# Loading the stacks of images 0 and 1 behind the last scores in a fused attention and convolution kernel

## The chip, the cores and the metric

The kernel runs on one core of one Trainium2 chip, as a single launch. The metric is the device time of a launch in microseconds (us), the median of several runs. All data are 32-bit floats.

## The reference

Two blocks follow each other on four images of 24 channels and 64 x 64 pixels. The first is a shifted-window transformer block with a gated convolution, the second a graph convolution with a small MLP.

```python
# x: (4, 24, 64, 64)
# block 1
xn  = layernorm over channels of x, gain norm1_g, shift norm1_b
q, k, v = windows of 8x8 of xn rolled by (-4, -4), 3 heads of 8 channels
att = softmax(q k^T / sqrt(8) + bias[rpb_table] + shift mask)
x   = x + unroll(att v @ proj_w.T + proj_b)
y   = layernorm over channels of x, gain norm2_g, shift norm2_b; its
      (positions, channels) are read on as (channels, rows, columns)
y   = conv1x1(y, pin_w)                  # 24 -> 126
y   = depthwise conv3x3(y, dw_w)         # padded by zeros
y   = gelu(y[:63]) * y[63:]
x   = x + conv1x1(y, pout_w)             # 63 -> 24
# block 2
h   = bn(conv1x1(x, w1))
xj  = max(0, h - rolls of h by even steps along rows, along columns)
h   = gelu(bn(conv1x1(concat(h, xj), wg)))
h   = bn(conv1x1(h, w2)) + x
out = conv1x1(gelu(conv1x1(h, wf1)), wf2)
```

## The kernel before

The kernel is written engine by engine: each engine has its own stream of instructions in a fixed order, and semaphores tie them. Its time has three stages, attention, convolution and the second block.

**Attention** runs over eight chunks m = 0 to 7 of 512 positions of all four images. Each chunk has four tiles t = 4m to 4m + 3. For a tile TensorE makes the scores (L595), VectorE adds the bias and takes the row maxima (L1065, L1069), GpSimd subtracts them (`subtract_max`, L496), TensorE transposes (`turn`, L606), ScalarE takes the exponential (L893) and TensorE multiplies by the values (`mix`, L624). Per chunk there follow the transposed output (L634), its projection (`project`, L641) and the residual. The second layer norm of chunk m runs some two chunks later: `turn_x1(m)` on TensorE (L578), `centre(1, m)` and `variance(1, m)` on VectorE, the square and the root on ScalarE (L930, L933), `gain(m)` (L453) and `second_norm(m)` (L466, L471) on GpSimd. For chunks 6 and 7 GpSimd takes the root itself with a power (L462), and VectorE's `variance(1, 7)` waits for the power of chunk 6.

The normalised chunk goes from SBUF to `scratch` in DRAM (`store_y(m)`, L273 or L275 to L277); the residual goes into the tile `x1` (`store_x1(m)`). Chunks 2b and 2b + 1 hold image b.

**Convolution.** `pin_w` and the 3 x 3 taps are folded into one product over a stack of shifted copies of an image: 12 channels times nine shifts are 108 partitions, and two stacks, sta and stb, hold the 24 channels. `load_stack(b, h)` loads half h of image b from scratch, with three DMAs into sta and three into stb (L292). A copy shifted in this way has wrong values at the image's borders, and GpSimd sets those to zero (`edges(b, h)`, L484): it waits for sta, multiplies three strips by 0 or 1, then the same for stb. `convolve(u)` on TensorE takes u = 8b + c, chunk c of image b (L650 on sta, L651 on stb); before u = 0, 4, 8, 12 and so on it waits for the edges of that half. It also waits for `gate(u - 4)`, so that its PSUM bank is free: ScalarE's gelu (L968) and VectorE's product (L1192) read it. convolve(0) to convolve(3) lie between the last steps of attention. From u = 25 on `pout_w` and the first product of block 2 are mixed in.

Images 0 and 3 share the buffers of the stacks, so `load_stack(3, 0)` waits until four chunks are convolved. Image 2's stacks lie over tiles of attention, so its load waits for the last scores. SP issues all loads and stores of these stages in one queue, in the order in which its program is written; GpSimd's order is written by hand too. TensorE's own instructions are fetched through a DMA queue of their own, which the trace lists as q8.

**Second block.** It is a pipeline over eight chunks at the end and is not touched.

Of the kernel before, what the change touches and what calls it, by code (L numbers as in the profile page):

```python
# [22 lines left out]
NCH = NT // CH  # L23
# [42 lines left out]
def build(nc, xw, xt, feat, pack, out):  # L66
    scratch = nc.dram_tensor("scratch", [B, PAD + C * NT + PAD], F32, kind="Internal").ap()

    with ExitStack() as ctx:
# [156 lines left out]
        def chunk(buf, n):  # L226
            return buf[:, bass.ts(n, CH)]
# [31 lines left out]
        def store_y(queue, m):  # L259
            b, i = divmod(m, 2)  # L260
            queue.wait_ge(y_ready, m + 1)
            tokens = scratch[b, PAD:PAD + C * NT].rearrange("(t c) -> t c", c=C)

            def rows_of(row, groups):
                part = tokens[W * row:W * (row + 8 * groups)]
                return part.rearrange("(g p k) c -> p g (k c)", g=groups, k=TOK)

            def half_of(row):
                return tokens[W * row:W * (row + 4)].rearrange("(p k) c -> p (k c)", k=TOK)

            done = y_stored[i]
            if i:
                queue.dma_start(rows_of(32 - SHIFT, 4), ytok[:, 1]).then_inc(done, 16)  # L273
            else:
                queue.dma_start(rows_of(8 - SHIFT, 3), ytok[:, 0, 1:4]).then_inc(done, 16)  # L275
                queue.dma_start(half_of(H - SHIFT), ytok[0:64, 0, 0]).then_inc(done, 16)
                queue.dma_start(half_of(0), ytok[64:128, 0, 0]).then_inc(done, 16)  # L277

        def load_stack(queue, b, h, paced=False):

            half = NT // 2
            for n in range(2):
                c0, c1 = STACKS[n]
                for y in range(3):
                    if paced and (n or y):
                        at, before = divmod(3 * n + y - 1, 3)
                        queue.wait_ge(stack_in[at][b][h], 16 * (before + 1))
                    src = scratch[b]
                    off = PAD + (y - 1) * W - 1 + c0 * NT + half * h
                    src = bass.AP(src.tensor, src.offset + off, [[NT, c1 - c0], [1, 3], [half // 2, 2], [1, half // 2]])  # L290
                    dst = stack(n, b)[y:RS:3, half * h:half * h + half].rearrange("p (q n) -> p q n", q=2)
                    queue.dma_start(dst, src).then_inc(stack_in[n][b][h], 16)  # L292
# [35 lines left out]
        @block.sync  # L328
        def _(sp):
            p0, p1, p2, p3 = PACK_LOADS  # L330

            def load_tokens(m):
                if m >= RING:
                    sp.wait_ge(cen_ready, m - RING + 1)
                sp.dma_start(xtok[:, m % RING], xt[:, GR * C * m:GR * C * (m + 1)]).then_inc(x_in[m % RING], 16)

            def load_channels(m):
                if m >= RING:
                    sp.wait_ge(x1s_ready, m - RING + 1)
                sp.dma_start(xin[:, m % RING], chunk(xw, m)).then_inc(channels_in[m % RING], 16)  # L340

            def store_x1(m):
                b, i = divmod(m, 2)
                sp.wait_ge(x1s_ready, m + 1)
                for g in range(4):
                    src, r0 = x1s[C * g:C * g + C, i], 32 * i + 8 * g - SHIFT
                    lane = lane_at(b, 4 * i + g, 0)
                    dst = x1[32 * lane:32 * lane + C]
                    if m == 0 and g == 0:
                        sp.wait_ge(x1_zeroed, 1)  # L350
                    if r0 < 0:
                        sp.dma_start(dst[:, H - SHIFT:H], src[:, 0:SHIFT]).then_inc(x1_stored[i], 16)
                        sp.dma_start(dst[:, 0:8 - SHIFT], src[:, SHIFT:8]).then_inc(x1_stored[i], 16)
                    else:
                        sp.dma_start(dst[:, r0:r0 + 8], src).then_inc(x1_stored[i], 16)

            def wait_for_y(b):
                for par in range(2):
                    sp.wait_ge(y_stored[par], y_count(par, b))

            load_tokens(0)
            sp.dma_start(pk[:, p0:p1], pack[:, p0:p1]).then_inc(first_in, 16)
            sp.dma_start(xs[BC:KX, :, :], feat.rearrange("k (i n) -> k i n", i=2)).then_inc(rows_in, 16)
            load_tokens(1)
            sp.dma_start(pk[:, p1:p2], pack[:, p1:p2]).then_inc(rpb_in, 16)
            load_tokens(2)
            sp.dma_start(pk[:, p2:p3], pack[:, p2:p3]).then_inc(weights_in, 16)
            load_tokens(3)
            for m in range(RING):
                load_channels(m)  # L370
            sp.dma_start(bass.AP(scratch.tensor, 0, [[2 * PAD + C * NT, B], [PAD + C * NT, 2], [1, PAD]]),
                         feat[1:2, 0:2 * B * PAD].rearrange("o (b e n) -> (o b) e n", b=B, e=2))\
                .then_inc(pads_in, 16)

            for m in range(NCH):
                if m + RING < NCH:
                    load_tokens(m + RING)
                if m >= 3:
                    store_y(sp, m - 3)
                if m >= 2:  # L380
                    store_x1(m - 2)
                    if m + 2 < NCH:
                        load_channels(m + 2)
                if m in (4, 6):
                    if m == 4:
                        sp.wait_ge(pads_in, 16)
                    b = m // 2 - 2
                    wait_for_y(b)
                    load_stack(sp, b, 0, False)
                if m in (5, 7):  # L390
                    load_stack(sp, m // 2 - 2, 1, False)
            store_y(sp, 5)
            wait_for_y(2)
            sp.wait_ge(scores_made, 4 * NCH)
            load_stack(sp, 2, 0)
            store_x1(6)
            store_y(sp, 6)
            store_y(sp, 7)
            load_stack(sp, 2, 1)
            store_x1(7)  # L400
            wait_for_y(3)
            sp.wait_ge(conv_made, NCH // 2)
            load_stack(sp, 3, 0)
            sp.wait_ge(conv_made, NCH)
            load_stack(sp, 3, 1)

            place_near(sp, 1, (0, 1), near_in[1])
            for c in range(2, NCH):
                place_near(sp, c, range(B), near_in[c % NRING])
            store_last(sp, 0, (2, 3), last_stored)  # L410
            store_last(sp, 1, range(B), last_stored)
            sp.wait_ge(last_stored, 96)
            for par in range(2):
                sp.wait_ge(stored[par], 16 * B * (NCH // 2) - 32 * par)
# [3 lines left out]
        def _(pool):  # L418
# [57 lines left out]
            def edges(b, h):  # L476

                rows = slice(H // 2 * h, H // 2 * h + H // 2)
                for n in range(2):
                    image = stack(n, b).rearrange("k (h w) -> k h w", w=W)  # L480
                    pool.wait_ge(stack_in[n][b][h], 48)

                    def mask(part, side):
                        return g.tensor_scalar(part, part, wt("edge", side, side + 1), None, ALU.mult)  # L484

                    mask(image[:, (H - 1) * h, :], 2 + h).then_inc(bordered[n], 1)
                    pool.wait_ge(bordered[n], 2 * b + h + 1)
                    mask(image[:, rows, 0:1], 0)
                    mask(image[:, rows, W - 1:W], 1).then_inc(edged[n], 1)
# [16 lines left out]
            for m in range(NCH):  # L506
                last = m == NCH - 1
                subtract_max(4 * m + 3)
                if m + 2 < NCH:
                    first_norm(m + 2)  # L510
                if not last:
                    subtract_max(4 * m + 4)
                if m + 3 < NCH:
                    centre(m + 3)
                if last:
                    edges(0, 1)
                if m >= 2:
                    gain(m - 2)
                if not last:
                    subtract_max(4 * m + 5)  # L520
                    if m == 6:
                        edges(0, 0)
                    subtract_max(4 * m + 6)
                if m >= 2:
                    second_norm(m - 2)
            gain(6)
            second_norm(6)
            edges(1, 0)
            gain(7)
            second_norm(7)  # L530
            edges(1, 1)
            for b in (2, 3):
                for h in range(2):
                    edges(b, h)
# [883 lines left out]
```

## Time and profile before

| what | value |
|---|---|
| median of 3 runs | 241.37 us (240.9 to 242.24) |
| the profiled execution | 239.28 us |
| its span | 237.5 us |
| TensorE busy | 213.7 us, 90% |
| VectorE busy | 161.9 us, 68% |
| ScalarE busy | 136.9 us, 58% |
| GpSimd busy | 128.1 us, 54% |
| chain of work that ended last | TensorE 77%, VectorE 7%, issue 6%, GpSimd 3% |

The profile follows one execution from its first to its last instruction, the span; the launch has a little time around it. Busy shares are means over stages. The chain goes back from the last instruction to whatever released each one, so a line that stands in it set the end at that time. TensorE is the chain from about 117 us to 187 us with short exceptions.

### The profile page before, as it was taken

Reading aid. Unit: us, or ns where it says so; the run is one execution under the profiler, and the core shown is the slowest. Engines: PE = TensorE matmul, PEld = TensorE weight load, DVE = VectorE, ACT = ScalarE, POOL = GpSimd, SP = SyncE. Lnnn points to the kernel's source line nnn. Section 1 sums busy time; section 2 is a strip of 40 time slices with the busy share of each in tenths; the row PEclk is TensorE's granted clock in tenths of the full one; section 3 lists DMA queues with packets and bytes.
Section 4 is the critical chain, followed back from the end, with each engine's and each line's share of the span. In section 5 each row is a group of like instructions: output and inputs, shape, how many; then the busy total and the mean of one; then the engine's idle time right before and its main releaser. Section 6 shows DMA issues by size and latency. Waiting matters only on the chain.

```text
span 237.5 us, 8554 instructions
## 1 busy us (share of the span) xinstructions
PE 213.7 (90%) x3618; PEld 111.0 (47%) x3618; DVE 161.9 (68%) x284; ACT 136.9 (58%) x225; POOL 128.1 (54%) x166
## 2 busy tenths in 40 slices
PE   7759799999999999987899999998999879999951
PEld 4326556575857677655555444443333223222220
DVE  4587999899898989794856734344368778655331
ACT  3547565686869596742435333332266643998970
POOL 8145746566988968675898992223400002245435
PEclk9999999999999999997999999999999988999997
DMA  5960000030120464574536366777300002254312
GB/s 169 273 149 3 3 4 4 11 97 3 36 73 27 111 230 111 164 234 154 185 91 257 118 229 196 226 225 236 124 3 0 4 0 58 62 118 92 77 33 66
DMA packets 12667, 25.27 MB, mean 106 GB/s; under 512 B 6697, under 2 KB 8193, under 8 KB 10902
## 3 DMA queue, kind: packets, MB, share of 16 engines
q1 hardware_dynamic: 11606, 23.21, 32.6%
q0 software_dynamic: 1024, 1.53, 2.8%
q8 instruction: 28, 0.46, 0.8%
q14 instruction: 9, 0.07, 0.1%
HBM read 18.63 MB, written 3.15 MB: 92 GB/s over the span
## 4 chain that ended last, share of the span: by engine, by line
PE 77%; DVE 7%; issue 6%; POOL 3%; ACT 2%; DMA 1%; SPq 1%; POOLq 0%; DVEq 0%; ACTq 0%
PE psum L650 12%; PE psum L651 12%; PE psum L595 10%; PE psum L606 6%; PE psum L624 5%; PE psum L818 3%; PE psum L797 3%; PE psum L555 3%; PE psum L775 3%; PE psum L641 3%; PE psum L551 3%; PE psum L788 2%; PE psum L562 2%; DVE biased L1065 2%; POOL diff L496 2%
## 5 line engine op out<-in xcount | busy, mean ns | idle before, releaser
L496 POOL TENSOR_TENSOR diff<-biased,mx 128x768 f32<-128x768 f32 x32 | 47.1, 1472 | 26.9 <-DVE mx L1069 26.0
L1192 DVE TENSOR_TENSOR gated<-psum,gel 64x512 f32<-64x512 f32 x32 | 22.1, 693 | 28.1 <-ACT gel L968 28.1
L1065 DVE TENSOR_TENSOR biased<-psum,pk 128x768 f32<-128x768 f32 x32 | 30.4, 951 | 10.9 <-PE psum L595 10.8
L893 ACT ACTIVATE pt<-psum 128x768 f32<-128x768 f32 x32 | 25.9, 808 | 18.6 <-PE psum L606 18.4
L968 ACT ACTIVATE gel<-psum 64x512 f32<-64x512 f32 x32 | 18.8, 590 | 30.7 <-PE psum L651 30.7
L650 PE MATMUL psum<-sta,pk 108*128 108x512 f32 x64 | 33.6, 607 | 0.9 <-issue 0.9
L651 PE MATMUL psum<-stb,pk 108*128 108x512 f32 x64 | 32.7, 592 | 0.0
L1069 DVE TENSOR_REDUCE mx<-biased 128x12 f32<-128x768 f32 x32 | 30.5, 953 | 1.1
L595 PE MATMUL psum<-kmv,stq 32*64 32x192 f32 x512 | 28.8, 340 | 2.6 <-DVE biased L1065 1.6
L314 POOL DMA_DIRECT2D out<-yo x28 | 14.0, 505 | 21.2 <-DVE yo L1289 21.2
L624 PEld LDWEIGHTS psum<-val,pt 128*32 128x32 f32 x1536 | 17.4, 112 | 12.5 <-issue 11.6
L624 PE MATMUL psum<-val,pt 128*32 128x18 f32 x1536 | 20.2, 188 | 2.8 <-issue 2.8
L606 PE MATMUL psum<-pk,diff 64*128 64x64 f32 x384 | 19.1, 234 | 2.8 <-POOL diff L496 2.6
L595 PEld LDWEIGHTS psum<-kmv,stq 32*64 32x64 f32 x512 | 16.6, 133 | 6.7 <-DVE biased L1065 2.9
L606 PEld LDWEIGHTS psum<-pk,diff 64*128 64x128 f32 x384 | 14.7, 141 | 10.2 <-issue 5.3
L651 PEld LDWEIGHTS psum<-stb,pk 108*128 108x128 f32 x64 | 12.2, 190 | 15.3 <-issue 15.3
L997 ACT ACTIVATE gf<-psum,small 96x1024 f32<-96x1024 f32 x16 | 16.9, 1104 | 4.1 <-PE psum L797 2.9
L650 PEld LDWEIGHTS psum<-sta,pk 108*128 108x128 f32 x64 | 11.3, 190 | 14.3 <-issue 14.3
L484 POOL TENSOR_SCALAR sta<-sta,pk 108x32 f32<-108x32 f32 (+1 forms) x24 | 9.7, 425 | 11.7 <-DMA sta<-scratch 10.9
L484 POOL TENSOR_SCALAR stb<-stb,pk 108x32 f32<-108x32 f32 (+1 forms) x24 | 9.7, 425 | 10.3 <-DMA stb<-scratch 9.5
L868 ACT ACTIVATE kmv<-psum,pk 128x512 f32<-128x512 f32 x21 | 13.7, 692 | 2.7 <-PE psum L555 2.5
L305 POOL DMA_DIRECT2D stb<-near x2 | 1.3, 630 | 25.1 <-DVE near L1224 25.1
(107 smaller groups left out, 355.8 us busy)
## 6 DMA issues: line engine op xcount, KB each, us to landing
sta<-scratch SPq DMA_DIRECT2D x24, 288.0 KB
stb<-scratch SPq DMA_DIRECT2D x24, 288.0 KB
xtok<-xt SPq DMA_DIRECT2D x8, 192.0 KB, 4.4
xin<-xw SPq DMA_DIRECT2D x8, 192.0 KB, 6.5
x<-x1s SPq DMA_DIRECT2D x28, 48.0 KB
out<-yo POOLq DMA_DIRECT2D x28, 48.0 KB, 2.0
pk<-pack SPq DMA_DIRECT2D x1, 827.5 KB, 8.9
scratch<-ytok SPq DMA_DIRECT2D x4, 192.0 KB, 4.8
```

What stands on the lines that cost most here:

```text
L484: return g.tensor_scalar(part, part, wt("edge", side, side + 1), None, ALU.mult)
L496: g.tensor_tensor(diff[:, t % 2].rearrange("q g w n -> q (g w) n"), scores_of, mx[:, t % 2].unsqueeze(2).to_broadcast([128, 4 * NH, WT]), ...
L595: l = mm(tile[:, w], stq[rows, m % 2, WT * n:WT * n + WT], kmv[rows, m % 2, n], start=True, stop=True)
L606: l = nc.tensor.transpose(bank(2 + j)[:, WT * k:WT * k + WT], diff[rows, t % 2, k].rearrange("p w n -> p (w n)"), wt("eye", 64 * j, 64 * j ...
L624: x = mm(o[32 * c:32 * c + 32, at:at + VW], pt[:, t % 2, c // 2, WT * k + 32 * (c % 2):WT * k + 32 * (c % 2) + 32], val[:, m % 2, l, p, c ...
L650: mm(bank(u % 4), wca, chunk(stack(0, b), c), start=True, stop=False)
L651: mm(bank(u % 4), wcb, chunk(stack(1, b), c), start=False, stop=True).then_inc(conv_made, 1)
L893: a(pt[:, t % 2], turned_banks, ACT.Exp).then_inc(probs_ready, 1)
L968: a(gel[:, u % 4, :], bank(u % 4)[0:64], ACT.Gelu).then_inc(gelu_ready, 1)
L1065: v.tensor_tensor(biased[:, slot].rearrange("q (p s) -> q p s", p=2), banks, wt("rpb").unsqueeze(1).to_broadcast([128, 2, 2 * NH * WT]), A ...
L1069: v.tensor_reduce(mx[:, slot], biased[:, slot].rearrange("q (g n) -> q g n", n=WT), AX.X, ALU.max)\
L1192: v.tensor_tensor(gated[64 * (b % 2):64 * (b % 2) + 64, b // 2, c * CH:(c + 1) * CH], bank(u % 4)[64:128], gel[:, u % 4, :], ALU.mult).the ...
```

## The change

It concerns the order of two programs. On SP, `load_stack(0, 1)`, `load_stack(1, 0)` and `load_stack(1, 1)` are moved from inside the loop over chunks to behind it: after `store_y(5)` and a wait for the last scores. The stores of chunks 6 and 7 lie between the later loads in another order. On GpSimd, `edges(0, 1)` moves from behind the last `subtract_max` to behind `second_norm(5)`, and `edges(1, 0)` from behind `second_norm(6)` to behind `second_norm(7)`. `load_stack(0, 0)` and `edges(0, 0)` stay.

```diff
-                if m in (4, 6):
-                    if m == 4:
-                        sp.wait_ge(pads_in, 16)
-                    b = m // 2 - 2
-                    wait_for_y(b)
-                    load_stack(sp, b, 0, False)
-                if m in (5, 7):
-                    load_stack(sp, m // 2 - 2, 1, False)
+                if m == 4:
+                    sp.wait_ge(pads_in, 16)
+                    wait_for_y(0)
+                    load_stack(sp, 0, 0)
             store_y(sp, 5)
+            sp.wait_ge(scores_made, 4 * NCH)
+            load_stack(sp, 0, 1)
+            wait_for_y(1)
+            load_stack(sp, 1, 0)
+            store_x1(6)
+            load_stack(sp, 1, 1)
             wait_for_y(2)
-            sp.wait_ge(scores_made, 4 * NCH)
             load_stack(sp, 2, 0)
-            store_x1(6)
             store_y(sp, 6)
+            store_x1(7)
             store_y(sp, 7)
             load_stack(sp, 2, 1)
-            store_x1(7)
             wait_for_y(3)
             sp.wait_ge(conv_made, NCH // 2)
             load_stack(sp, 3, 0)
```

```diff
                 if m + 3 < NCH:
                     centre(m + 3)
-                if last:
-                    edges(0, 1)
                 if m >= 2:
                     gain(m - 2)
...
                 if m >= 2:
                     second_norm(m - 2)
+            edges(0, 1)
             gain(6)
             second_norm(6)
-            edges(1, 0)
             gain(7)
             second_norm(7)
-            edges(1, 1)
+            for h in range(2):
+                edges(1, h)
             for b in (2, 3):
                 for h in range(2):
                     edges(b, h)
```

## Rows read from the trace of the kernel before

**Rows 1.** The page, busy tenths of the engines in 40 slices of the span.
```profile
PE   7759799999999999987899999998999879999951
```

**Rows 2.** The chain that ended last: start us, us, what.
```profile
91.50 1.03 PE psum L641 x2
...
104.33 1.03 PE psum L641 x2
...
119.68 1.04 PE psum L641 x2
...
130.03 0.89 PE psum L650 x2
...
136.93 0.86 PE psum L650 x2
```

**Rows 3.** Timeline of TensorE: start us, us, instructions, idle time before and its releaser.
```profile
108.64 0.30 PE L624 MATMUL psum<-val,pt 128*32 128x18 f32 x3 [2.78 <-issue]
108.86 0.91 PE L606 MATMUL psum<-pk,diff 64*128 64x64 f32 x12
...
165.31 1.10 PE L650 MATMUL psum<-sta,pk 108*128 108x512 f32 x2 [0.91 <-issue]
```

**Rows 4.** DMA queue q8 at 99 to 99.5 us, then at 106 to 106.5 us.
```profile
q8 instruction: 1, 0.02, 11.9%
...
q8 instruction: 1, 0.02, 13.6%
```

**Rows 5.** Timeline of SP's queue: start us, us, DMAs.
```profile
95.30 2.37 SPq L292 DMA_DIRECT2D sta<-scratch  x3
...
107.38 2.36 SPq L292 DMA_DIRECT2D sta<-scratch  x3
...
121.95 2.36 SPq L292 DMA_DIRECT2D sta<-scratch  x3
...
126.71 0.51 SPq L273 DMA_DIRECT2D scratch<-ytok  x1
132.79 2.35 SPq L292 DMA_DIRECT2D sta<-scratch  x3
...
156.54 2.32 SPq L292 DMA_DIRECT2D sta<-scratch  x3
```

**Rows 6.** Windows: busy us by engine; last three columns clock, DMA share, GB/s.
```profile
105.00:106.00 1.00, 0.86 (x46) 0.47 (x45) 0.96 (x2) 0.06 (x1) 0.91 (x1) 1.00 0.83 250
...
108.00:113.00 5.00, 4.36 (x103) 3.38 (x107) 1.79 (x3) 1.60 (x4) 2.27 (x6) 0.66 0.57 185
...
116.00:117.00 1.00, 0.94 (x46) 0.76 (x50) 0.90 (x3) 0.58 (x2) 1.00 (x2) 1.00 0.29 98
```

**Rows 7.** Timeline of GpSimd.
```profile
109.15 1.31 POOL L484 TENSOR_SCALAR stb<-stb,pk 108x64 f32<-108x64 f32 x3
113.35 1.47 POOL L496 TENSOR_TENSOR diff<-biased,mx 128x768 f32<-128x768 f32 x1 [2.89 <-DVE mx L1069]
...
121.77 0.83 POOL L466 TENSOR_TENSOR cen<-gained,rstd 128x384 f32<-128x384 f32 x1
...
123.74 1.02 POOL L453 TENSOR_TENSOR gained<-cen,pk 128x384 f32<-128x384 f32 x1
125.14 2.93 POOL L462 TENSOR_TENSOR rstd<-var,power 128x16 f32<-128x16 f32 x1 [0.38 <-DVE var L1048]
...
130.06 1.31 POOL L484 TENSOR_SCALAR sta<-sta,pk 108x64 f32<-108x64 f32 x3
...
132.56 1.01 POOL L453 TENSOR_TENSOR gained<-cen,pk 128x384 f32<-128x384 f32 x1
...
137.61 1.02 POOL L471 TENSOR_TENSOR ytok<-cen,pk 128x384 f32<-128x384 f32 x1
...
144.66 1.31 POOL L484 TENSOR_SCALAR stb<-stb,pk 108x64 f32<-108x64 f32 x3 [2.23 <-DMA stb<-scratch]
...
170.76 1.31 POOL L484 TENSOR_SCALAR stb<-stb,pk 108x64 f32<-108x64 f32 x3 [1.84 <-DMA stb<-scratch]
```

**Rows 8.** Timeline of ScalarE.
```profile
120.76 0.22 ACT L933 ACTIVATE rstd<-logs 128x16 f32<-128x16 f32 x1
```

**Rows 9.** Waits of SP's queue: us in total, times, longest us.
```profile
SPq L394 <- DMA scratch<-ytok: 5.5, 1, 5.5
```

## The prediction

> **What bounds the kernel now.** I read first the slices of the page [rows 1]: TensorE is nearly full from slice 17 to slice 31 but for a dip at slices 17 to 20. The chain of work that ended last shows what sets each piece of the end, and TensorE's timeline, the windows and the DMA view show what happens in the dip.
>
> In attention the chain repeats itself: L641, the project of one chunk, starts at 91.50 and 12.83 us later at 104.33. The next starts at 119.68, 15.35 us later [rows 2]. In between TensorE stands still for 2.78 us, inside one mix: the last 3 of its 48 products start at 108.64, behind "issue", not behind another engine [rows 3]. Its instruction queue, q8, has one packet at 99 to 99.5 us and the next not before 106 to 106.5 [rows 4], at the end of the traffic of load (0,1) (image 0, half 1), which SP issues from 95.30 on [rows 5]; the DMA engines are 0.83 busy in microsecond 105 [rows 6]. I read the hole as an instruction fetch that the stack load held up.
>
> From convolve(4) at 130.03 the chain is TensorE alone; convolve(8) starts at 136.93 [rows 2], four chunks in 6.90 us. One hole is left, 0.91 us before convolve(24) at 165.31 [rows 3], where the stack masks come late. Beside it GpSimd is busy from 121.77 to 138.6 with the last second norms and masks [rows 7]. So from 130 us on TensorE is the bound, and GpSimd's work is hidden while it keeps ahead of it.
>
> **The change part by part.** *SP.* Three loads of six DMAs each go back in SP's queue: (0,1) issued from 95.30, (1,0) from 107.38, (1,1) from 121.95 [rows 5]. A load takes SP 4.76 us to issue (121.95 to the store at 126.71 [rows 5]). They now stand behind store_y(5), so (0,1) can't start before chunk 5 is normalised. The queue ahead of it only gets shorter. The wait for the last scores costs nothing: TensorE makes them before chunk 5 is centred.
>
> *Gain in attention.* Without (0,1) at 95 to 106 the fetch comes in time. The transposes that started at 108.86 [rows 3] could then follow the mix at about 105.9. Next comes GpSimd: its masks of (0,0) end at 109.15 + 1.31 = 110.46, where subtract_max(30) started at 113.35 [rows 7]: 2.9 us stay. The masks of (0,1) leave GpSimd's queue ahead of gain(5), but second_norm(5) waits for ScalarE's root, done at 120.76 + 0.22 = 120.98 [rows 8], so that gives only 121.77 - 120.98 = 0.8 us. Chunk 5 was ready when gain(6) began, at 123.74 [rows 7]; now it is at 123.7 - 0.8 - 2.9 = 120.0. Call this A.
>
> *The new wait.* Behind A come in series: 0.5 us for SP to issue the store of chunk 5, then L, from the first DMA of load (0,1) to the landing of stb. Three sizes of L are in the rows. Load (1,0), issued at 107.38 [rows 5] with little behind it, is over where the DMA share has fallen to 0.29, in microsecond 116 [rows 6]: at some 116.3, 8.9 us. Load (2,0), with stores and a load behind it, is issued at 132.79 [rows 5] and its stb mask starts at 144.66, on the landing [rows 7]: 11.8. Load (3,1), in a full queue, has its DMAs of sta issued from 156.54, and its masks of stb start at 170.76 [rows 5, 7]: 14.2. Here load (1,0) follows at once, so I take 11.8, with 8.9 and 14.2 as ends.
>
> Then the stb masks, 1.31 us. GpSimd stands at edges(0,1) all this time. Queued behind are gain and norm of chunks 6 and 7 and the masks of (1,0). Chunk 6 takes 123.74 to 130.06, less 0.38 of waiting before its power: 5.94. Chunk 7 takes 132.56 to 137.61 + 1.02: 6.07. The masks of (1,0) take 130.06 to 132.56 and the overlap with gain(7): 2.57 [rows 7].
>
> convolve(4) then starts at 120.0 + 0.5 + 11.8 + 1.3 = 133.6, where TensorE was ready at 130.03 - 2.9 = 127.1: a stall of 6.5 us. It is swallowed by a second: convolve(8) waits for edges(1,0), 133.6 + 5.94 + 6.07 + 2.57 + 0.1 = 148.3, where TensorE would be ready at 133.6 + 6.9 = 140.5. Before it started at 136.93 [rows 2]: +11.4 us.
>
> VectorE's variance(1,7) waits for GpSimd's power of chunk 6, now at 137.6, and gate(4) is queued behind it; convolve(8) is the first to wait for gate(4), so this costs nothing.
>
> *The clock.* After the 2.78 us hole the granted clock is 0.66 over 108 to 113 [rows 6], so 0.34 x 5 = 1.7 us of work at full speed (2.4 GHz) is lost in a dip to the lower level (1.2 GHz). Of the two new stalls the first has over 7 us of slack behind it and its dip costs nothing; the second costs 1.7. The ends are 0 and 3.4, twice the row.
>
> *Later loads.* (1,0) is issued at 125 to 130 and must be down by 145.6. (1,1) is due for convolve(12) at 155, (2,0) for convolve(16) at 162; issued from 134 and 139 they are down at about 146 and 151 by the same L. Further on I take the stream as a whole: from 132.79 to 170.76 [rows 5, 7] it carried four loads (each six DMAs of 288 KB) and four stores of 192 KB, 7.9 MB in 38.0 us, 207 GB/s. Now seven loads and five such stores, 13.4 MB, follow A. (3,0) is down at 176 and masked at 177.4, where convolve(24) stands at 165.31 + 12.2 = 177.5. (3,1) is masked at 186; convolve(28) needs it near 188. So the stream costs nothing, barely, and today's hole before convolve(24) isn't paid again: -0.9.
>
> Sum: +11.4 + 1.7 - 0.9 = +12.2 us. The profiled execution took 239.28 us (a span of 237.5 and 1.8 around it) and would take 251.5. The median of the runs shown, 241.37, is 2.1 above the profiled one; the forecast is 241.37 + 12.2 = 253.6 us.
>
> The Trainium skill, "DMA: Bandwidth & Descriptors", section "Queues, rings and completion order", says that each DMA engine takes the descriptors of one issuing engine's ring in order. By that the loads behind (0,1) wouldn't hold it up, L would be 8.9 and the sum 250.7. The trace rather speaks against it: (2,0) took 11.8 us although the queue ahead of it was empty, SP having just waited 5.5 us for the last store to land [rows 9].
>
> **The rivals.** *R1, the hole isn't the loads'.* The fetch may come late for another reason, such as a burst of short instructions. For it: the trace shows when q8's packet moved, not why it started then. Against it: 7 us between two fetches, and both the long gap and the hole lie right under load (0,1). Then A is 122.9, all is 2.9 later, and the time 256.5. The Trainium skill, "Runtime: NRT & Kernel Launch", section "Instruction fetch mechanics", calls the cost of streaming instructions in blocks mostly hidden, which would speak for this rival.
>
> *R2, the short landing.* L is 8.9 us, as for (1,0), and the time 250.7. For it: what is behind a load in the queue needn't slow it. Against it: the 11.8 us of (2,0).
>
> *R3, the stream becomes the bound.* If seven loads in a row move 10% slower than 207 GB/s, (3,0) is masked at 183.8, 6.3 us after convolve(24) could start: 259.9. For it: the 14.2 us of (3,1). Against it: the 207 GB/s are a mean over a stretch just like it, SP's waits included.
>
> *R4, not slower.* Attention gets faster by far more than the hole, because the loads slow all of it. This decides if chunk 5 is ready at 107.8 or before, 12.2 us before A; the time would be 240 or less. Against it: the chunk from 91.50 to 104.33, under most of load (0,1), took 12.83 us [rows 2], and all that is left from 104.33 to A is 15.7 us.
>
> **How the numbers follow.** Forecast 0.56, R1 0.18, R2 0.16, R3 0.06, R4 0.04. The low end is R2 without the clock's cost, 250.7 - 1.7 = 249.0. The high end is R1 with L half way to 14.2 (+1.2) and half the clock's upper end (+0.8), 258.5. A measurement of this kernel tells about 0.5% (1.2 us) from no change. All cases but R4 lie far above that: slower 0.96, same 0.01, faster 0.03.
>
> **What the profile after would show.** Right: no hole inside the mix, and chunk 5 normalised at about 120; GpSimd idle for some 10 us before the first masks of (0,1), released by a DMA; TensorE still before convolve(4), and again for 6 to 8 us before convolve(8), which starts near 148; the lower clock for some 3 us behind the stall; no hole before convolve(24). Wrong: the hole stays (R1); stb's masks of (0,1) start under 10 us after the first issue (R2); holes before convolve(24) or (28) (R3); convolve(8) at 137 or earlier (R4).

## The result, and the profile after

The changed kernel takes 252.18 us (median of 4 runs, 251.27 to 253.39), the kernel before 241.13 us (4 runs, 237.71 to 242.24). The ratio is 1.054, with a 95% interval of 1.039 to 1.069. The ratio stands for 12.9 us, the difference of the medians for 11.05. Executions of one kernel fall into faster and slower ones, the slower with a lower granted clock: ratios in this document compare the faster ones alone, medians take in all, and the profiles of two experiments (e6 and e9 in the table below) are of slower ones. The forecast was 253.6 us, from 249.0 to 258.5, slower with 0.96. The profiled execution took 251.27 us, with a span of 249.5 us; the forecast on the old execution's scale was 251.5.

One thing must be read otherwise than in "The kernel before": a chunk of attention is 2048 positions, half of one image, not 512 positions of all four. So load (0,1) needs chunks 0 and 1 alone, and SP issues its first DMA at 95.30 [rows 5] in the kernel before. The change makes it wait for chunk 5, whose data it doesn't read.

TensorE's timeline of the changed kernel shows two stalls, before convolve(4) and before convolve(8). L649 and L650 are the lines of the two stacks now.

```profile
105.31 0.88 PE L594 MATMUL psum<-kmv,stq 32*64 32x192 f32 x16
106.12 1.10 PE L640 MATMUL psum<-mt,pk 97*96 97x512 f32 x2
107.15 0.61 PE L623 MATMUL psum<-val,pt 128*32 128x18 f32 x48
107.68 0.58 PE L605 MATMUL psum<-pk,diff 64*128 64x64 f32 x12
...
127.86 0.60 PE L577 MATMUL psum<-pk,x1s 96*128 96x96 f32 x4
133.93 2.05 PE L649 MATMUL psum<-sta,pk 108*128 108x512 f32 x2 [5.47 <-issue]
135.77 1.91 PE L650 MATMUL psum<-stb,pk 108*128 108x512 f32 x2
...
148.19 2.05 PE L649 MATMUL psum<-sta,pk 108*128 108x512 f32 x2 [5.21 <-issue]
150.03 1.76 PE L650 MATMUL psum<-stb,pk 108*128 108x512 f32 x2
151.62 1.02 PE L649 MATMUL psum<-sta,pk 108*128 108x512 f32 x2
```

The mix at 107.15 runs all its 48 products in one piece, and the transposes follow at once: the hole of [rows 3] is gone. The profile writes "issue" at both new stalls, since it doesn't name the releaser. The times do: GpSimd's timeline answers to [rows 7].

```profile
117.04 1.02 POOL L453 TENSOR_TENSOR gained<-cen,pk 128x384 f32<-128x384 f32 x1
119.48 0.83 POOL L466 TENSOR_TENSOR cen<-gained,rstd 128x384 f32<-128x384 f32 x1 [1.42 <-ACT rstd L932]
120.40 1.02 POOL L471 TENSOR_TENSOR ytok<-cen,pk 128x384 f32<-128x384 f32 x1
128.85 1.32 POOL L484 TENSOR_SCALAR sta<-sta,pk 108x64 f32<-108x64 f32 x3 [7.43 <-DMA sta<-scratch]
132.51 1.32 POOL L484 TENSOR_SCALAR stb<-stb,pk 108x64 f32<-108x64 f32 x3 [2.34 <-DMA stb<-scratch]
133.76 1.02 POOL L453 TENSOR_TENSOR gained<-cen,pk 128x384 f32<-128x384 f32 x1
134.74 2.94 POOL L462 TENSOR_TENSOR rstd<-var,power 128x16 f32<-128x16 f32 x1
...
144.52 1.01 POOL L471 TENSOR_TENSOR ytok<-cen,pk 128x384 f32<-128x384 f32 x1
145.51 1.32 POOL L484 TENSOR_SCALAR sta<-sta,pk 108x64 f32<-108x64 f32 x3
146.77 1.31 POOL L484 TENSOR_SCALAR stb<-stb,pk 108x64 f32<-108x64 f32 x3
```

GpSimd is ready for the masks of (0,1) at 121.42 and stands for 7.43 + 2.34 = 9.8 us until both stacks have landed. Then come two norms without a gap, and the masks of (1,0) end at 148.08, just before convolve(8) at 148.19. So each stall ends with a mask.

SP's queue shows the load going out right behind the store of chunk 5, the answer to [rows 5]:

```profile
82.52 2.38 SPq L292 DMA_DIRECT2D sta<-scratch  x3
...
121.45 0.36 SPq L273 DMA_DIRECT2D scratch<-ytok  x1
121.86 2.37 SPq L292 DMA_DIRECT2D sta<-scratch  x3
```

Windows of the changed kernel, with the granted clock, the DMA share and the GB/s as the last columns:

```profile
15.00:25.00 10.00, 8.26 (x171) 5.01 (x174) 6.67 (x8) 5.21 (x12) 4.42 (x3) 0.83 0.08 26
...
134.00:138.00 4.00, 4.00 (x5) 1.75 (x6) 0.22 (x1) 0.28 (x1) 3.92 (x3) 0.52 0.75 242
...
148.00:152.00 4.00, 3.81 (x5) 1.70 (x6) 0.00 (x0) 0.18 (x1) 2.42 (x7) 0.57 0.83 257
```

Behind each stall TensorE is granted about half its full clock. The first line is a dip at the start, where the two kernels are the same. In the profile before, the same stretch reads 1.00:

```profile
15.00:25.00 10.00, 7.84 (x232) 5.42 (x234) 8.07 (x10) 6.41 (x15) 6.04 (x5) 1.00 0.10 30
```

Load (0,0) is issued at 82.52 instead of 80.58, 1.9 us later. Of the 13 profiles in this document, nine have this dip and issue load (0,0) at 82.05 to 84.00; four have none and issue it at 80.53 to 80.75. Nothing that the change moves has run by then. But all nine have another order on SP than the kernel before, and of the four only e7 has, so whether the dip is chance or comes with the change is open. To take this out I measure a middle stretch from here on. It runs from the first DMA of load (0,0) to the product L719 (L720 before) that waits for the residual of chunk 7, the first row below; the second is the same row of the kernel before:

```profile
201.26 0.67 PE L719 MATMUL psum<-gated,pk 64*32 64x256 f32 x16 [1.11 <-DVE x L1235]
```

```profile
80.58 2.38 SPq L292 DMA_DIRECT2D sta<-scratch  x3
189.27 0.67 PE L720 MATMUL psum<-gated,pk 64*32 64x256 f32 x16 [1.11 <-DVE x L1236]
```

The middle takes 189.27 - 80.58 = 108.7 us before and 201.26 - 82.52 = 118.7 after, 10.05 us more. What follows takes 48.2 us in both. So of the 12.0 us between the two spans, 1.9 are the start and 10.05 what the moved loads and masks cost.

The 10.05 us depend on which profile of the kernel before is taken. A second one (last experiment) has a hole of 1.12 us in place of 2.78 and a middle of 105.3 us; against it they cost 13.4 us. The 12.9 us of the ratio lie between the two. All other kernels have one profile each, so a difference of less than some 3 us in the middle stretch shows nothing by itself.

### The profile page after: what moved, and what is told of

It is laid out like the page before. It is cut to its first block and busy times, and to the rows that moved or that the text cites. A ratio compares the mean times of both kernels' runs of the same rounds, so it can differ in the third digit from the quotient of the medians.

```text
span 249.5 us, 8554 instructions
## 1 busy us (share of the span) xinstructions
PE 215.2 (86%) x3618; PEld 111.1 (45%) x3618; DVE 161.7 (65%) x284; ACT 137.1 (55%) x225; POOL 128.3 (51%) x166
## 5 line engine op out<-in xcount | busy, mean ns | idle before, releaser
L649 PE MATMUL psum<-sta,pk 108*128 108x512 f32 x64 | 35.7, 641 | 10.7 <-issue 10.7
L650 PE MATMUL psum<-stb,pk 108*128 108x512 f32 x64 | 34.3, 619 | 0.0
L649 PEld LDWEIGHTS psum<-sta,pk 108*128 108x128 f32 x64 | 12.1, 204 | 25.2 <-issue 24.9
L623 PEld LDWEIGHTS psum<-val,pt 128*32 128x32 f32 x1536 | 16.9, 110 | 9.2 <-issue 9.0
L650 PEld LDWEIGHTS psum<-stb,pk 108*128 108x128 f32 x64 | 12.7, 199 | 16.5 <-issue 16.5
L623 PE MATMUL psum<-val,pt 128*32 128x18 f32 x1536 | 19.5, 187 | 0.0
```

Source lines behind the costliest of these rows:

```text
L623: x = mm(o[32 * c:32 * c + 32, at:at + VW], pt[:, t % 2, c // 2, WT * k + 32 * (c % 2):WT * k + 32 * (c % 2) + 32], val[:, m % 2, l, p, c ...
L649: mm(bank(u % 4), wca, chunk(stack(0, b), c), start=True, stop=False)
L650: mm(bank(u % 4), wcb, chunk(stack(1, b), c), start=False, stop=True).then_inc(conv_made, 1)
```

## The experiments

The middle stretch, worked out from the profile of each kernel in the same way, beside the median times. The kernel before was run beside each and had medians of 240.2 to 241.5 us.

| kernel | median us | middle us |
|---|---|---|
| before | 241.13 | 108.7 |
| before, second profile | one run of 236.70 | 105.3 |
| changed | 252.18 | 118.7 |
| GpSimd's order alone (e1) | 246.21 | 113.4 |
| changed, edges(1,0) back (e2) | 249.47 | 114.2 |
| changed, chunk 6's norm first (e3) | 252.02 | 117.8 |
| changed, SP waits behind (0,1) (e5) | 251.58 | 119.3 |
| changed, (0,1) alone late (e9) | 259.15 | 128.1 |
| before, image 1 alone late (e8) | 244.70 | 112.6 |
| before, (0,1) behind (0,0) (e4) | 244.57 | 110.4 |
| before, each load a chunk later (e7) | 242.77 | 106.6 |
| before, loads cut by stack (e6) | 239.94 | 108.2 |
| before, (0,1) in chunk 6 (e10) | 244.50 | 108.7 |

### GpSimd's order alone

```diff
-                if last:
-                    edges(0, 1)
...
+            edges(0, 1)
             gain(6)
             second_norm(6)
-            edges(1, 0)
             gain(7)
             second_norm(7)
-            edges(1, 1)
+            for h in range(2):
+                edges(1, h)
```

> The kernel before with GpSimd's new order alone: edges(0,1) behind second_norm(5), edges(1,0) behind second_norm(7); SP's queue as before. Theory (the cost is the landing of (0,1), and GpSimd's order only decides what is queued behind it): without a wait for the landing the order shifts masks among norms; edges(1,0) ends some 2 us after convolve(8) could start (chunk 7's norm ends at about 136.1, masks at 138.7, against 136.93), so +1 to +3 us on the kernel before. The hole in the mix near 106 us stays, since load (0,1) is still issued at 95. Rival (the order on GpSimd is itself the cost): +8 us or more. Rival R1 (the hole isn't the loads') expects the hole too, and says nothing else here.

The ratio to the kernel before is 1.024 (1.015 to 1.033), 5.7 us by it: more than the +1 to +3 expected. The place was right and the price too small. TensorE's timeline and the chain:

```profile
107.63 0.24 PE L623 MATMUL psum<-val,pt 128*32 128x18 f32 x3 [1.88 <-issue]
...
139.35 2.04 PE L649 MATMUL psum<-sta,pk 108*128 108x512 f32 x2 [3.41 <-issue]
```

```profile
139.35 2.04 PE psum L649 x2
141.40 1.71 PE psum L650 x2
143.10 1.71 PE psum L649 x2
144.81 1.40 PE psum L650 x2
```

convolve(8) starts at 139.35, 2.4 us later than before, as forecast. But two chunks then take 146.21 - 139.35 = 6.86 us, where two at full clock take 3.43. This stall costs 3.4 us of clock, twice what I took from [rows 6], and as much again as the stall itself. So GpSimd's order is a cost even with an early load: close to half of the whole (5.7 of 12.9 us by the ratios, 4.7 of 10.05 in the middle stretch). The hole is there too, 1.88 us.

### The changed kernel with edges(1,0) put back

```diff
             second_norm(6)
+            edges(1, 0)
             gain(7)
             second_norm(7)
-            for h in range(2):
-                edges(1, h)
+            edges(1, 1)
```

> The changed kernel with edges(1,0) put back between second_norm(6) and gain(7). Theory (convolve(8) waits because chunk 7's norm, 5.9 us, stands ahead of the masks of (1,0)): load (1,0) lands at about 140 to 142, its masks end at about 142 to 143.5, TensorE is ready at 142.8; the 5.2 us stall and the 1.9 us of lower clock behind it go nearly or wholly: 5 to 7 us faster than the changed kernel, about 246 us. Rival (the landing of (1,0) comes late too, 145 or after, since loads behind one another slow down): at most 2 us faster.

2.7 us faster than the changed kernel by the medians, 4.6 in the middle stretch and 4.3 by the shortest runs (246.96 against 251.27), where 5 to 7 were expected. The timeline of TensorE shows that the second stall is gone, and what took its place:

```profile
133.16 2.05 PE L649 MATMUL psum<-sta,pk 108*128 108x512 f32 x2 [4.98 <-issue]
149.96 1.10 PE L649 MATMUL psum<-sta,pk 108*128 108x512 f32 x2 [0.62 <-issue]
165.41 1.10 PE L649 MATMUL psum<-sta,pk 108*128 108x512 f32 x2 [1.47 <-issue]
```

The 5.2 us before convolve(8) fell away with their lower clock. Two small holes came, before convolve(12) and convolve(20). The theory holds: chunk 7's norm ahead of the masks of (1,0) made the second stall. Some of the gain goes to the next limit, the loads.

### The changed kernel with chunk 6's norm in the idle time

```diff
-            edges(0, 1)
             gain(6)
             second_norm(6)
+            edges(0, 1)
```

> The changed kernel with gain(6) and second_norm(6) put ahead of edges(0,1), into the 10 us in which GpSimd stands idle. Theory (idle GpSimd at edges(0,1) pushes both norms behind the landing): convolve(4) still starts at about 133.9; chunk 7's norm ends at about 139.8, the masks of (1,0) at 142.4, and convolve(8) starts at 142.4 to 143: 5 to 7 us faster than the changed kernel, about 246 us. Rival (convolve(8) is bound by the landing of (1,0) or by the stream of loads): at most 2 us faster; holes before convolve(24) or (28) would then show.

The median is 252.02 us, 0.2 under the changed kernel, and the middle 0.95 us shorter. The ratio to the kernel before is 1.047 (1.034 to 1.060) against 1.054 for the changed kernel, so the gain is not clear of noise. It is not the 5 to 7 us of the theory: here the rival was right. TensorE's timeline:

```profile
133.69 2.05 PE L649 MATMUL psum<-sta,pk 108*128 108x512 f32 x2 [5.39 <-issue]
150.34 1.10 PE L649 MATMUL psum<-sta,pk 108*128 108x512 f32 x2 [0.67 <-issue]
157.60 1.10 PE L649 MATMUL psum<-sta,pk 108*128 108x512 f32 x2 [0.16 <-issue]
167.54 1.14 PE L649 MATMUL psum<-sta,pk 108*128 108x512 f32 x2 [2.84 <-issue]
```

The stall before convolve(8) is gone, as the theory says. But TensorE then comes to convolve(20) early and waits 2.84 us for (2,1), whose stb masks start at 166.13 on the landing, and the clock dips behind that. In the changed kernel convolve(20) started at 170.67, and the same masks at 165.36. So behind GpSimd's queue the stream of loads was the next limit, with 4 us of slack, and a faster GpSimd ran into it.

### A wait on SP behind load (0,1)

```diff
             load_stack(sp, 0, 1)
+            for n in range(2):
+                sp.wait_ge(stack_in[n][0][1], 48)
             wait_for_y(1)
```

> The changed kernel in which SP waits until load (0,1) has landed before it issues load (1,0). It measures L, the time from the first DMA of load (0,1) to the landing of stb, with nothing behind it; it was 10.65 us in the changed kernel. Theory of the forecast (loads behind it slow it): L falls to about 8.9 us and convolve(8) starts 1.7 us earlier, 1.7 us faster unless (1,0), issued 6 us later, lands after 145.5. Rival R2's reason (one ring is served in order): L stays within 0.5 us of 10.65, and nothing is gained. In either case the later start of the stream of loads may show as a hole before convolve(24) or convolve(28), up to 4 us.

L is 10.09 us here, from 122.29 to the stb masks:

```profile
122.29 2.37 SPq L292 DMA_DIRECT2D sta<-scratch  x3
```

```profile
132.38 1.31 POOL L486 TENSOR_SCALAR stb<-stb,pk 108x64 f32<-108x64 f32 x3 [2.06 <-DMA stb<-scratch]
```

That is 0.56 us less than the 10.65 of the changed kernel. Two more profiles have SP's queue as in the changed kernel and give L as 131.75 - 121.56 = 10.19 us (e2) and 132.28 - 121.70 = 10.58 (e3), so even the 0.56 is hardly clear of scatter: what is queued behind load (0,1) slows it by some 0.6 us at most here. Here R2's reason was right and mine wrong. Its size was not: even alone the load takes 10.1 us, not 8.9. The windows show why:

```profile
131.40:131.60 0.20, 0.00 (x0) 0.00 (x0) 0.00 (x0) 0.00 (x0) 0.00 (x0) 0.50 0.10 41
131.60:132.30 0.70, 0.00 (x0) 0.00 (x0) 0.00 (x0) 0.00 (x0) 0.00 (x0) 0.50 0.00 0
```

The DMA engines have nothing left to do from about 131.5 on, 9.2 us after the first issue, and GpSimd's mask starts 0.9 us after that. The 8.9 us of the prediction were read at the end of the traffic, the 11.8 and 14.2 at the start of the mask. Nor do the 11.8 us of (2,0) come from what stood behind it: up to 141.39 that was 192 KB of `x1` in five DMAs, less than the whole load behind (0,1) in the changed kernel. What made it longer stays open. By the rule of the Trainium skill named in the prediction ("DMA: Bandwidth & Descriptors", "Queues, rings and completion order") nothing behind would count at all, and the trace agrees within that scatter. The time is that of the changed kernel, and the later stream made no hole.

### Load (0,1) alone late

```diff
                     load_stack(sp, 0, 0)
+                if m in (6, 7):
+                    if m == 6:
+                        wait_for_y(1)
+                    load_stack(sp, 1, m - 6)
             store_y(sp, 5)
             sp.wait_ge(scores_made, 4 * NCH)
             load_stack(sp, 0, 1)
-            wait_for_y(1)
-            load_stack(sp, 1, 0)
             store_x1(6)
-            load_stack(sp, 1, 1)
```

> The changed kernel with image 1 loaded early again: (1,0) and (1,1) in chunks 6 and 7 as before, (0,1) alone behind the last scores; GpSimd's order as changed. Theory (convolve(8) starts at the landing of (0,1) + 1.3 for its stb masks + 11.9 for two norms + 2.6 for the masks of (1,0)): load (0,1) now stands behind (1,1) and the store of chunk 5, is issued at about 127 and lands at 137 to 138; convolve(4) starts at 139, convolve(8) at 153 to 154, and the whole is 4 to 6 us slower than the changed kernel, 256 to 258. The early loads of image 1 gain nothing. Rival (the late loads of image 1 are the cost, as all traffic then comes at once): faster than the changed kernel by 3 us or more.

259.15 us, 1 above what the theory gave and far from the rival. With more loaded early the kernel is 7 us slower than the changed one, since (0,1) now stands behind (1,1): it is issued at 125.94, 4.1 us later, and takes 15.25 us to land, 4.6 longer. GpSimd and TensorE:

```profile
141.19 1.31 POOL L485 TENSOR_SCALAR stb<-stb,pk 108x64 f32<-108x64 f32 x3 [3.23 <-DMA stb<-scratch]
```

```profile
142.60 2.04 PE L650 MATMUL psum<-sta,pk 108*128 108x512 f32 x2 [14.37 <-issue]
156.84 2.05 PE L650 MATMUL psum<-sta,pk 108*128 108x512 f32 x2 [4.74 <-issue]
```

From the landing of (0,1) to the start of convolve(8) it is 156.84 - 141.19 = 15.65 us. In the changed kernel it is 148.19 - 132.51 = 15.68, in e5 148.03 - 132.38 = 15.65. The forecast had 16.0 for this chain. Two landings 8.7 us apart (132.51 and 141.19) move convolve(8) one for one: that chain sets it.

### Image 1 alone late

```diff
+                if m == 5:
+                    load_stack(sp, 0, 1)
             store_y(sp, 5)
+            wait_for_y(1)
+            load_stack(sp, 1, 0)
+            load_stack(sp, 1, 1)
```

Load (0,0) stays in chunk 4, the other two loads leave the loop.

> The kernel before with (1,0) and (1,1) moved behind store_y(5); (0,1) stays in chunk 5 and GpSimd's order is as before. Theory: no stall before convolve(4); (1,0) is issued at 127 and lands at 137, its masks end at 138.5, so convolve(8) starts 1 to 2 us late, with up to 2 us for the clock; six loads in a row from 127 at 207 GB/s would have (3,1) down at about 183 against 176, so that holes of 1 to 5 us come before convolve(20), (24) or (28). In all 2 to 7 us slower than the kernel before, and 4 us or more faster than the changed kernel. The hole in the mix near 106 stays. Rival (image 1's loads are most of the cost): within 2 us of the changed kernel.

The ratio is 1.027 (1.018 to 1.037), or 6.5 us; by the medians it is 4 us over the kernel before beside it and 7.5 under the changed one. Both are in the expected range. The hole in the mix is 3.05 us here, and the late stream shows as holes of 0.55, 1.28, 0.96 and 1.12 us before convolve(8), (12), (20) and (24); the one before convolve(12) was not expected, and no lower clock stands behind any. So the late loads of image 1 cost four tenths to half of the whole by themselves.

### Load (0,1) right behind (0,0)

```diff
                     load_stack(sp, b, 0, False)
+                    if m == 4:
+                        load_stack(sp, 0, 1)
-                if m in (5, 7):
+                if m == 7:
                     load_stack(sp, m // 2 - 2, 1, False)
```

> The kernel before with one move: load (0,1) is issued in chunk 4 right behind load (0,0), at about 85 instead of 95 us. Theory (the hole in the mix near 106 us is an instruction fetch held up by the load): nothing moves 1.7 MB at 99 to 107 us any more, the hole goes, attention ends 2.9 us earlier, and with the lower clock behind it 2 to 5 us are gained on the kernel before, unless the traffic, now at 81 to 100 us, holds up another fetch. Rival R1 (the fetch is late for another reason): the hole of 2 to 3 us near 106 stays and the time is that of the kernel before within 1 us.

It is slower than the kernel before, by 1.021 (1.007 to 1.035). The hole near 106 us is gone, so R1 falls. But two came instead. The packets of q8 ahead of them are at 93.1 and 99.7 us, both within the traffic as it now lies, which ends at about 101:

```profile
95.79 0.45 PE L626 MATMUL psum<-val,pt 128*32 128x18 f32 x33 [0.93 <-issue]
...
102.75 1.26 PE L597 MATMUL psum<-kmv,stq 32*64 32x192 f32 x14 [1.55 <-issue]
```

The clock fell to 0.50 after the second. Here moving a load moved the hole.

### Milder forms

Three kernels look for an order that has the hole no more and keeps the stream early. In the first, each load comes one chunk later:

```diff
+                if m == 6:
+                    load_stack(sp, 0, 1)
+                if m == 7:
+                    wait_for_y(1)
+                    load_stack(sp, 1, 0)
             store_y(sp, 5)
+            load_stack(sp, 1, 1)
```

> A milder form of the change: the kernel before with each load one chunk later, (0,1) in chunk 6, (1,0) in chunk 7, (1,1) behind store_y(5); GpSimd's order as before. Theory: (0,1) is issued at about 105 and down at 115, before GpSimd asks for it at 118; (1,0) from 120 is down at 130, as GpSimd asks; (1,1) is issued at 127 and all later loads follow one load later, so the stream (207 GB/s, 8.5 us a load) is late for convolve(20) or (24) by 2 to 6 us. The hole of 2.8 us at 106 goes, another may come under (0,1) at 108 to 115. In all -2 to +4 us on the kernel before. Rival (loads inside attention cost nothing but the one hole, and the stream has slack): 3 us or more faster.

In the second the loads are cut by stack, three DMAs in a burst:

```diff
+                if m == 5:
+                    load_stack(sp, 0, 1, parts=(0,))
+                if m == 6:
+                    load_stack(sp, 0, 1, parts=(1,))
+                    wait_for_y(1)
+                    load_stack(sp, 1, 0, parts=(0,))
+                if m == 7:
+                    load_stack(sp, 1, 0, parts=(1,))
+                    load_stack(sp, 1, 1, parts=(0,))
             store_y(sp, 5)
+            load_stack(sp, 1, 1, parts=(1,))
```

> The kernel before with the loads cut by stack: sta of (0,1) in chunk 5, its stb and sta of (1,0) in chunk 6, stb of (1,0) and sta of (1,1) in chunk 7, stb of (1,1) behind store_y(5). Bursts in attention are three DMAs long until chunk 6. Theory (a burst under which a fetch falls makes the hole): the hole near 106 shrinks below 1 us or goes, since sta's three DMAs are down by 101; up to 3 us faster than the kernel before, unless the later stb of (1,1) pushes the stream back (2.4 us at most, seen before convolve(24)). Rival (the holes only move): holes of the same sum elsewhere, time within 1.5 us of the kernel before or above it.

In the third (0,1) alone moves, to chunk 6 just ahead of (1,0), and all else stays:

```diff
+                    if m == 6:
+                        load_stack(sp, 0, 1)
                     wait_for_y(b)
                     load_stack(sp, b, 0, False)
-                if m in (5, 7):
-                    load_stack(sp, m // 2 - 2, 1, False)
+                if m == 7:
+                    load_stack(sp, 1, 1)
```

> The kernel before with (0,1) alone one chunk later, in chunk 6 just ahead of (1,0); all else as before. Theory: the hole near 106 goes with the traffic at 97 to 106; the twelve DMAs from 106 on are down by 124, so (0,1) lands before GpSimd asks for it at about 116 to 118 or up to 2 us late, and from (1,1) on the stream is as before, so that no more than the 0.9 us hole before convolve(24) comes back. 0 to 4 us faster than the kernel before, unless another fetch falls under the traffic of 106 to 124. Rival (each load put under attention holds up some fetch wherever it stands): a hole of 1 to 3 us at 108 to 122, and no gain.

None beats the kernel before: medians of 242.77 against 240.67 us beside it, 239.94 against 240.67 (ratio 0.996, 0.989 to 1.004), and 244.50 against 241.50 (1.011, 0.999 to 1.023). In all three profiles the hole near 106 us is gone. What came in its place is the stream, in TensorE's timeline of each:

```profile
155.52 1.10 PE L652 MATMUL psum<-sta,pk 108*128 108x512 f32 x2 [0.94 <-issue]
163.40 1.10 PE L652 MATMUL psum<-sta,pk 108*128 108x512 f32 x2 [0.78 <-issue]
```

```profile
158.81 1.10 PE L656 MATMUL psum<-sta,pk 108*128 108x512 f32 x2 [2.14 <-issue]
166.50 1.10 PE L656 MATMUL psum<-sta,pk 108*128 108x512 f32 x2 [0.58 <-issue]
```

```profile
160.24 1.10 PE L652 MATMUL psum<-sta,pk 108*128 108x512 f32 x2 [1.88 <-issue]
168.75 1.10 PE L652 MATMUL psum<-sta,pk 108*128 108x512 f32 x2 [1.41 <-issue]
```

TensorE is done with attention earlier and waits before convolve(20) and (24) instead. In e10 these holes add up to 3.3 us, where at most the 0.9 us before convolve(24) was expected. Its rival was right that there is no gain, but not in its reason: in the first and the third profile load (0,1) runs from 106 or 109 us on, and no hole of 0.25 us or more stands under it. So not every load in attention holds TensorE up. In the second, sta's half of (0,1) at 95.52 makes no hole near 106 either.

### The kernel before once more

> The kernel before unchanged, for a second profile. Theory (load (0,1) holds up a fetch): a hole of 1.5 to 3 us in TensorE's work near 106 us, with the gap between two packets of its instruction queue 6 us or more. If the hole of the first profile was an accident of that execution, there is none here.

The single run took 236.70 us. Its hole stands at the same place but is 1.12 us long, with no dip of the clock:

```profile
107.11 0.24 PE L624 MATMUL psum<-val,pt 128*32 128x18 f32 x3 [1.12 <-issue]
```

```profile
104.00:114.00 10.00, 7.95 (x247) 5.41 (x243) 9.17 (x17) 3.88 (x8) 9.03 (x12) 1.00 0.60 173
```

Over the same 10 us the first profile was granted 0.83. Here the next packet of TensorE's instruction queue came at 104.5, 5.5 us after the last, not at 106.0. I had expected 1.5 us or more of hole and 6 us or more between the packets: it repeats in place, not in size. The two go together in all four profiles that have this hole: the packet is at 106.0 (first profile), 105.3 (e1), 108.0 (e8) and 104.5 us, and the mix goes on 2.3 to 2.6 us later, at 108.64, 107.63, 110.61 and 107.11. The size of the hole may well be part of the spread of the kernel before, 236.0 to 243.8 us over its runs, but only two of those executions have a profile.

## Why the prediction was right

Term by term, with the start's 1.94 us taken off the times of the changed kernel:

| step | forecast | measured |
|---|---|---|
| chunk 5 normalised (A) | 120.0 | 121.42 - 1.94 = 119.5 |
| store of chunk 5, then first DMA | 0.5 us | 0.44 us |
| L | 11.8 us | 10.65 us |
| landing to convolve(8) | 16.0 us | 15.68 us |
| convolve(8) starts | 148.3 | 148.19 - 1.94 = 146.25 |
| against 136.93 [rows 2] | +11.4 us | +9.3 us |
| lower clock behind it | +1.7 us | 151.79 - 148.19 - 1.72 = +1.9 us |
| hole before convolve(24) | -0.9 us | gone, -0.9 us |
| sum | +12.2 us | +10.3 us, +10.05 over the middle |

**The gain in attention** was right: the hole went, and from the first DMA of (0,0) to chunk 5 it takes 38.9 us, against 123.7 - 80.58 = 43.1 before: 4.2 us for the forecast 3.7. e4, e6, e7 and e10 show that the hole goes when the load goes, so R1 falls. That a late instruction fetch is what TensorE waits for fits the packets of q8, 7 us apart there before and 4 to 5 after, and the mix that goes on 2.3 to 2.6 us behind the packet in four profiles. But no run took the fetch alone away. It is argued, not shown.

**The new wait** was right in its mechanism: e9 and e5 show convolve(8) following the landing, e2 that chunk 7's norm is in the chain. The term that was mis-sized is L, 11.8 for 10.65, since I took the loads behind it to slow it; e5 puts their share at 0.56 us, about the scatter of L between profiles. The row it was taken from, (2,0), had less behind it than (0,1) has in the changed kernel, and why it took 11.8 is open. R2 had the reason, but its 8.9 us was too short, read at the end of the traffic and not at the mask, some 1 us later. The true L lies between the two.

**The first stall is free,** as forecast: 5.47 us before convolve(4) and its lower clock are swallowed by the second. The second was 5.21 us, where 6 to 8 were forecast: L, the first stall and its dip all came out other than forecast.

**The clock** cost 1.9 us for 1.7. That this was close was partly luck: in e1 a shorter stall cost 3.4.

**The stream** was no bound (R3). It ran from 121.86 to 178.74 with seven loads and four stores, 13.2 MB in 56.9 us, 232 GB/s, where I had taken 207 from a stretch in which SP had also waited. With 207, (3,0) would have come in the very moment it was needed; its stb masks started at 172.46, 5 us ahead of convolve(24) at 177.54. e3 shows that this slack is used up once GpSimd's order is mended.

**R4** fell: convolve(8) came 9.3 us late, and attention got only 0.5 us faster than the hole and the masks explain.

The forecast of 253.6 us was 1.4 above the median. The measured size of the change is 10 us in the profile, 11.05 between the medians and 12.9 by the ratio; 12.2 was forecast. Most of the 2 us between forecast and profile is L (1.15) and A (0.5), the rest the norms and masks (0.3). That the profiled time came so near the forecast, 251.27 for 251.5, was luck: 1.9 us of it is the dip at the start, which no term has, and it makes up for the terms that were too long. The 0.5% that the prediction gave as what a measurement can tell was too small: the interval of the ratio is 1.5% to either side.

## What to carry to other kernels

A load that is moved behind a stage brings its landing time with it, and the engine that waits for it in a fixed order brings its whole queue: here 10.7 us of landing and 11.8 us of norms stood in series, with TensorE behind. Count from the last thing the load now waits for to the first that needs it, and everything queued behind that wait. A stall removed from one place was in the main paid at the next limit (e3, e7), so look for the second limit before a first one is mended.

## What was not expected of the hardware

- Holes of 1.1 to 3.05 us stand in TensorE's work, behind "issue", at the same mix in the four profiles where load (0,1) was issued at 95.3 to 97.7 us (2.78, 1.12, 1.88 and 3.05), though TensorE doesn't use its data there. There is none of 0.25 us or more at that mix in the nine others. With load (0,1) at 87 us there were two elsewhere (0.93 and 1.55, e4), and two profiles have a small one under load (0,0) (0.67 at 89.71 in e5, 0.77 at 89.97 in e6). Other loads under attention made none of 0.25 us or more, save one of 0.34 at 117.41 in e4.
- The price of a stall in clock varies widely: 3.4 us after 3.41 us of standing still, 1.9 after 5.21, none after 1.12. Two holes of 1.88 us had different ends: 0.83 over the 10 us of 106 to 116 in e1, 1.7 us lost, and a full clock behind the one at 160.24 in e10.
- A load of six DMAs of 288 KB took 10.1 us from first issue to the mask it releases with nothing behind it, and 10.2 to 10.65 with another load right behind it. What stands ahead in the queue counts: it took 15.3 us when issued 5.75 us behind another load (125.94 to 141.19 in e9).
